# Attention behind two expert layers: when the transposes and the copy of a group's row maxima are issued

## The reference, cut to what matters

```python
x = L0_attn_x                                    # (1, 2048, 512) float32
x = x + 0.5 * _L0_ffn_ref(_layernorm(x), ...)    # 8 experts, top 2
x = x + _L0_attn_ref(_layernorm(x), wq, wk, wv, wo)
x = x + 0.5 * _L0_ffn_ref(_layernorm(x), ...)

# _L0_attn_ref: QH = 16 heads of HD = 32, KVH = 4 heads of keys and values
q = apply_rope(q, cos, sin); k = apply_rope(k, cos, sin)
attn = jnp.einsum('bhqd,bhkd->bhqk', q, k) / np.sqrt(HD)
mask = jnp.triu(jnp.ones((t, t), dtype=bool), k=1)
attn = jnp.where(mask[None, None], -jnp.inf, attn)
attn = jax.nn.softmax(attn, axis=-1)
out = jnp.einsum('bhqk,bhkd->bhqd', attn, v)
```

## Time and profile before

| | before |
|---|---|
| median of three runs | 1295.05 us |
| the three runs | 1291.39, 1296.23, 1295.05 us |
| the profiled execution's own time | 1291.39 us |
| its span | 1290.1 us |
| TensorE matmuls busy | 1198.4 us, 93% |
| TensorE weight loads busy | 778.3 us, 60% |
| VectorE busy | 891.7 us, 69% |
| ScalarE busy | 665.4 us, 52% |
| GpSimd busy | 599.7 us, 46% |
| mean granted TensorE clock | 0.987 of full |

### The profile page before, as it was taken

One profiled execution on the slowest core, in us unless ns is written; L12 is line 12 of the kernel. 1 busy time (PEld: TensorE's weight loads), 2 busy tenths in 40 slices (PEclk: granted clock), 3 DMA queues, 4 the chain that ended last, 5 costly groups with the idle time before them and its releaser, 6 DMA issues.

```text
span 1290.1 us, 22099 instructions
## 1 busy us (share of the span) xinstructions
PE 1198.4 (93%) x7406; PEld 778.3 (60%) x7413; DVE 891.7 (69%) x2100; ACT 665.4 (52%) x1321; POOL 599.7 (46%) x496
## 2 busy tenths in 40 slices
PE   4899999999998999999999999989999978999996
PEld 3578888758776555444545455545444446777774
DVE  7767777679996666476577677677763666666664
ACT  2545555436555554354456565456567853444442
POOL 4845444323210111001436457454764273888886
PEclk9899999999999999999999999999999999999998
DMA  9933333565630032023445844655843263666665
GB/s 331 364 97 107 106 108 108 169 178 107 101 57 5 32 68 35 1 69 67 98 99 147 173 108 99 197 120 146 162 98 67 69 236 85 102 106 101 101 103 78
DMA packets 68557, 148.52 MB, mean 115 GB/s; under 512 B 8832, under 2 KB 29312, under 8 KB 64448
## 3 DMA queue, kind: packets, MB, share of 16 engines
q0 software_dynamic: 35184, 93.34, 34.3%
q1 hardware_dynamic: 33264, 53.77, 12.2%
HBM read 81.28 MB, written 33.55 MB: 89 GB/s over the span
## 4 chain that ended last, share of the span: by engine, by line
PE 61%; DVE 15%; DMA 10%; issue 6%; POOL 4%; ACT 4%; SPq 0%; DVEq 0%; POOLq 0%; ACTq 0%
PE bank L839 10%; PE bank L1635 10%; PE bank L1647 9%; PE bank L997 8%; PE bank L862 6%; PE bank L1702 4%; PE bank L1665 4%; DMA XG<-xn,TK 4%; POOL out L789 3%; DMA out<-Y,DI 3%; DVE PM L1010 3%; DVE bank L1012 2%; PE bank L821 2%; PE bank L1398 2%; DMA CD<-P 1%
## 5 line engine op out<-in xcount | busy, mean ns | idle before, releaser
L1754 ACT ACTIVATE P<-bank 128x512 f32<-128x512 f32 (+3 forms) x640 | 303.6, 535 | 259.3 <-PE bank L1635 252.7
L1010 DVE TENSOR_REDUCE PM<-bank 128x1 f32<-128x512 f32 x384 | 252.8, 686 | 82.6 <-PE bank L997 81.9
L1635 PE MATMUL bank<-Qs,Ks 98*128 98x512 f32 (+3 forms) x640 | 241.0, 407 | 5.1 <-ACT P L1754 2.8
L997 PE MATMUL bank<-Ks,Qs 96*128 96x512 f32 (+3 forms) x640 | 234.4, 387 | 10.8 <-DVE PM L1012 5.3
L1635 PEld LDWEIGHTS bank<-Qs,Ks 98*128 98x128 f32 x640 | 116.8, 190 | 130.8 <-issue 59.5
L1813 POOL TENSOR_SCALAR_AFFINE_SELECT P<-P 128x512 f32<-128x512 f32 x64 | 42.7, 677 | 284.6 <-ACT P L1754 235.2
L1012 DVE CUSTOM_DVE_ANT_0 bank<-bank,KB 128x128 f32<-128x128 f32 (+3 forms) x256 | 124.7, 499 | 56.4 <-PE bank L997 55.8
L997 PEld LDWEIGHTS bank<-Ks,Qs 96*128 96x128 f32 x640 | 121.5, 191 | 57.5 <-DVE PM L1010 17.5
L1647 PE MATMUL bank<-P,V 128*32 128x512 f32 (+3 forms) x1280 | 150.9, 543 | 3.7 <-POOL P L1813 3.7
L1827 POOL TENSOR_TENSOR CH<-CH,P 128x512 f32<-128x512 f32 x108 | 139.2, 1435 | 14.1 <-ACT P L1754 13.3
L789 POOL DMA_INDIRECT out<-Y,DI x78 | 126.1, 1617 | 38.4 <-issue 29.4
(11 more groups left out here) (195 smaller groups left out, 1978.1 us busy)
## 6 DMA issues: line engine op xcount, KB each, us to landing
CD<-P POOLq DMA_DIRECT2D x17, 1024.0 KB, 7.3
xn<-XN SPq DMA_DIRECT2D x8, 1024.0 KB, 6.5
WR<-L_ffn_w POOLq DMA_DIRECT2D x16, 512.0 KB, 15.6
XO<-y POOLq DMA_DIRECT2D x8, 1024.0 KB, 9.6
WR<-L_ffn_w SPq DMA_DIRECT2D x16, 512.0 KB, 8.4
CD<-P SPq DMA_DIRECT2D x7, 1024.0 KB, 5.2
CD<-CH POOLq DMA_DIRECT2D x7, 1024.0 KB, 6.9
XA<-y POOLq DMA_DIRECT2D x24, 256.0 KB, 4.2
```

Of the source, the lines that this page charges most:

```text
L997: pe.matmul(bk(g, bank)[:, 0:n], g.Qs[b][0:96, G % 4 * 4 + h, c * P:c * P + P], g.Ks[0:96, G % 4, k * BQ:k * BQ + n], start=True, stop=Tru ...
L1010: dve.tensor_reduce(dst, bk(g, bank)[:, 0:n], AX.X, ALU.max).then_inc(s(f"free{bank}"), 1)
L1635: pe.matmul(bk(g, bank)[:, o:BQ], g.Ks[0:98, G % 4, k * P:k * P + P], g.Qs[G // 4][0:98, G % 4 * 4 + j, o:BQ], start=True, stop=True).then ...
L1754: act.activation(a.P4[buffer_of(n)][:, j, o:BQ], bk(g, score_bank(g, i))[:, o:BQ], ACT.Exp, scale=scale).then_inc(s("exp"), 1)
```

## The change

A group's transposes (`found`) are issued one place later: not behind the weigh at j = 3, but at j = 0 of the next tile, behind its first score and the tops that stand there. The copy (`foundcopy`) is issued one score further on, at j = 1. VectorE's `solvemax` stays where it was.

```diff
-    told, weight, given, extra, known, copying, free = 4, 0.0, 0.0, [], [], [], True
+    told, weight, given, extra, known, solved, turned, free = 4, 0.0, 0.0, [], [], [], [], True
@@
-            if copying:
-                plan.append(("foundcopy", copying.pop()))
+            if turned:
+                plan.append(("foundcopy", turned.pop()))
+            if solved:
+                turned.append(solved.pop())
+                plan.append(("found", turned[0]))
             if j == 1 and extra:
                 plan += extra.pop(0)
             if j == 3 and n:
                 if known and known[0][0] <= at and free and n - 1 not in LAST.values():
-                    copying.append(known.pop(0)[1])
-                    plan.append(("solvemax", copying[0]))
+                    solved.append(known.pop(0)[1])
+                    plan.append(("solvemax", solved[0]))
                 plan.append(("weigh", n - 1))
-                if copying:
-                    plan.append(("found", copying[0]))
```

## The result

The changed kernel's median is 1287.93 us (9 runs, 1285.94 to 1292.19) against 1295.05 us before, 7.1 us less. The ratio on record, which is estimated from all runs of both kernels and is not the ratio of the two medians (0.9945), is **0.9962, interval [0.9945, 0.9980]**, 4.9 us. So by the three readings the change makes the kernel faster by 0.1 to 0.4%, 1.5 to 4.9 us. The first shows the largest gain, and the third by itself can't be told from no change.

What follows compares the result with a forecast made beforehand. TensorE was taken to bound the attention stage, gaining only where it stands still. Cover 2.95, copy waits 0.7, group 6 -0.1 and group 8 0.8 sum to 4.35 us: 1295.05 - 4.35 = 1290.7 us, own range 1289 to 1293.

Steps and rivals of the forecast that it cites:

- the range that I gave 8 times in 10: Whole kernel: the median of the changed kernel lies between 1285.5 and 1296.5 us.
- the clock's rival: Behind group 8: less idling removes a fall of TensorE's clock, 1.7 us more gained, 1287 to 1289 us; chance 0.20.
- the sum of 4.35: Attention stage: all terms together, 2.95 + 0.7 - 0.1 + 0.8 us, taken off the time before.
- The cover of the wait: Groups 9 to 14: score and tops ahead of the transposes fill TensorE's wait for VectorE's maxima, 2.95 us.
- the two copy waits at groups 9 and 12: TensorE's wait for ScalarE's copy to free the transposes' bank goes there, 0.35 us each, 0.7 together.
- group 8's 0.8: Group 8: the 512-wide top ahead of the router's transpose goes out earlier and VectorE's chain moves up, 0.8 us.
- group 15's 0.18: Group 15: 0.18 us of covered wait, struck from the sum because TensorE soon waits 1.20 us for GpSimd.
- The wait itself: TensorE's transposes waiting for VectorE's last step of the maxima: from 5.8 to about 2.7 us, in five places.
- Groups 4 to 7 at nothing: No wait for the maxima to win there; copy waits at 5 and 7 stay, group 6 loses 0.1 us.
- Group 10's 0.35: Group 10: a score and the narrow top cover 0.35 of the 0.82 us wait for the maxima.
- Nothing gained: TensorE runs ahead but loses the gain waiting for banks VectorE has not freed; 1294 us, chance 0.20.
- The held-back copy: Twelve groups: copy behind two exponentials frees the bank 0.54 us later each, 6.5 us in all, 1297.2 us; chance 0.05.

Runs made afterwards that it cites:

- the three readings: The changed kernel against the kernel before, measured three times: ratios 0.9962, 0.9985 and 0.9988.
- the old place and the close copy: Kernel before with the transposes left behind the weigh and the copy right behind them, ahead of the next tile's first exponential: ratio 0.9967.
- the close copy: Changed kernel with the copy right behind the moved transposes, behind the tile's first exponential and not its second: ratio 0.9953 to the kernel before.

## Why the prediction was right, and where not

The median of 1287.93 us lies in the range that I gave 8 times in 10, but below my own range of the forecast, 1289 to 1293, and in the band of the clock's rival, 1287 to 1289. That rival is not what happened: the profiled executions of both kernels have 10.2 us at the low clock in the attention stage, and that stage is 4.3 us shorter, as the sum of 4.35 said. The other 3 us of the difference of the medians are not explained by the change, I call them luck, and so is how near the first ratio (4.9 us) comes to the sum, for the next two readings give 1.9 and 1.6 us. What bears the prediction out is the comparison place by place.

The time from solve to solve, from profiles in which the clock did not fall in that stretch ("fall" marks the one for which there was none such; the forecast is my term for the place):

| stretch | before, us | changed, us | difference | forecast |
|---|---|---|---|---|
| first score to group 4's solve | 31.41 | 31.50, 31.48 | +0.1 | 0 |
| 4 to 5 | 27.54 | 27.77 | +0.23 | 0 |
| 5 to 6 | 31.49 | 31.25 | -0.24 | 0 |
| 6 to 7 | 46.65 | 46.93 | +0.28 | +0.1 |
| 7 to 8 | 44.18 | 44.36 | +0.18 | 0 |
| 8 to 9 | 53.72 | 52.80 | -0.92 | -0.8 |
| 9 to 10 | 40.99 | 40.12 | -0.87 | -0.92 |
| 10 to 11 | 42.65, 42.68, 42.91 | 44.45, 44.51, 45.93 (fall) | +1.8 or more | -0.35 |
| 11 to 12 | 50.95 | 50.48 | -0.47 | -0.48 |
| 12 to 13 | 65.61 | 64.67 | -0.94 | -0.94 |
| 13 to 14 | 54.04 | 53.52 | -0.52 | -0.48 |
| 14 to 15 | 51.79 | 51.34 | -0.45 | -0.48 |
| 15 to the end | 28.93 | 28.94 | 0 | 0 |

Without the row of group 10 the differences sum to -3.6 us; the forecast's terms without that of group 10 sum to -4.0.

The mark itself moves a little at groups 4 to 8. VectorE's reduction writes into the bank that the transposes take, which is another one now. At group 5 the solve stands 1.15 us behind the start of the weigh beside it and stood 0.92 behind it before, at group 8 1.48 and 1.30. That the other bank comes free later is the likely cause and is not shown. From weigh to weigh instead of from solve to solve, the rows from 4 to 8 are +0.06, -0.08, +0.28 and +0.04, and that of group 8 is -0.74. From group 9 on the mark stands where it stood.

**The cover of the wait** held, place by place, within 0.05 us, but for group 10. So did the two copy waits at groups 9 and 12 (0.35 each, inside 0.92 and 0.94), and, within 0.1, group 8's 0.8. That group 15's 0.18 would be lost to GpSimd held too: the mask is waited for 1.23 us now, 1.20 before.

**The wait itself fell further than forecast**, to 1.6 us instead of 2.7. At group 12 it lost 0.78 us where the cover was put at 0.59. Half of the difference stands in the timeline: the score behind a weigh is followed only 0.34 us later (787.47 to 787.81), not 0.24. The first matmul behind one of another kind so takes 0.1 more until the next starts, and the change adds one such switch at each group: weigh, score, transposes, score instead of weigh, transposes, score. Where TensorE waits anyway the 0.1 is hidden in the wait. I took all added spacing for work done. The other half, some 0.1 us at groups 12 and 13, is open.

**Groups 4 to 7 at nothing was wrong by a little.** From weigh to weigh they cost 0.3 us together, where I had 0.1. With no wait to hide it, the added switch is paid, 0.1 at each. Against it stand the copy waits of groups 5 and 7, which I had expected to stay near 0.5: they were 0.56 and 0.26 us and are 0.29 and 0.21. Group 6's is 0.59 for 0.51. At group 4 there is also a new wait of 0.31 us, of the spread reciprocals for L1010:

```profile
453.41 1.08 PE L1683 MATMUL bank<-K,R 128*32 128x128 f32 x32 [0.31 <-DVE PM L1010]
```

These terms sum to nearly 0.5 and not to 0.3; the rest is open.

**Group 10's 0.35 was not seen in the end.** The step that failed there is the cover term of 0.35 us: I counted it in full, although a chain of transfers bounds the end of this stretch. GpSimd's additions by DMA for group 9 form a chain in which each waits for the landing of the one before. In the changed kernel, over this stretch:

```profile
685.21 0.86 POOL L1844 DMA_DIRECT2D CD<-P  x1 [0.84 <-ACT P L1755]
...
697.39 0.85 POOL L1844 DMA_DIRECT2D CD<-P  x1 [0.53 <-ACT P L1755]
...
710.53 0.86 POOL L1844 DMA_DIRECT2D CD<-CH  x1 [4.31 <-DMA CD<-P]
...
711.87 2.07 POOL L1814 TENSOR_SCALAR_AFFINE_SELECT P<-P 128x512 f32<-128x512 f32 x2
```

and in the kernel before:

```profile
689.73 0.86 POOL L1843 DMA_DIRECT2D CD<-P  x1 [0.82 <-ACT P L1754]
...
702.36 0.85 POOL L1843 DMA_DIRECT2D CD<-P  x1 [1.00 <-ACT P L1754]
...
714.67 0.86 POOL L1843 DMA_DIRECT2D CD<-CH  x1 [3.78 <-DMA CD<-P]
```

From the first to the last issue it is 25.3 us now and 24.9 before, though the middle issue, which waits for ScalarE and not for a transfer, comes 0.45 us sooner. The mask stands behind the last of them on GpSimd's queue, and TensorE behind the mask. So this stretch is bound by the landing of the middle transfer, and what TensorE wins ahead of it it waits out: 1.79, 1.82 and 1.82 us in the three profiles of the changed kernel, 1.83 with the change for groups 9 to 15 alone, against 1.26, 1.23 and 1.48 us before. I had checked this absorption for group 15 and not for group 10.

Why the middle transfer lands later though it is issued sooner shows in part. SyncE's load `XO<-L_attn_x`, also of 1 MB, stands behind the maxima's own two transfers on its queue and so behind the copy. It goes out at 697.50 now and 701.99 before, in both kernels 4.00 us behind group 10's solve, and the two transfers are under way together. The last number is the us from issue to landing, first of the changed kernel, then of the kernel before:

```profile
CD<-P POOLq DMA_DIRECT2D x1, 1024.0 KB, 12.6
XO<-L_attn_x SPq DMA_DIRECT2D x1, 1024.0 KB, 8.7
...
XO<-L_attn_x SPq DMA_DIRECT2D x1, 1024.0 KB, 6.5
CD<-P POOLq DMA_DIRECT2D x1, 1024.0 KB, 11.8
```

With the old place and the close copy the load goes out 3.29 us behind the solve; the addition is issued at 4.13, later than in the changed kernel (3.89), and yet lands 15.0 us behind the solve for 16.5, TensorE has no wait for the mask there, and the stretch takes 41.52. So in this stretch the copy's place seems to count more than the transposes', by way of this load. That is argued from these rows; no run moved the load alone.

**The clock was a rival that looked in the wrong place.** I looked for a fall that goes, behind group 8. What the profiles show is one that comes, behind group 10's longer stand:

```profile
712.00:713.00 1.00, 0.00 (x0) 0.00 (x0) 0.43 (x1) 0.19 (x1) 1.00 (x3) 1.00 1.10 213
713.00:714.00 1.00, 0.49 (x4) 0.23 (x8) 0.00 (x0) 0.00 (x0) 0.94 (x2) 0.71 1.05 213
...
716.00:717.00 1.00, 1.00 (x7) 0.78 (x4) 0.00 (x0) 0.26 (x2) 0.00 (x0) 0.58 1.06 115
```

TensorE stood still in the us from 712 and has the lower level from 713.4 to 716.8. A fall stands at this place in all five profiles in which group 10's transposes had moved and the copy stood one score behind (3.4, 3.4, 6.8 and 6.8 us long, and 10.2 with the solve moved too), and in none of seven with the transposes in their old place there. With the close copy the order there is the same up to the copy, the stand is 1.11 us, there is no fall, and the stretch takes 42.00; one score further the stand is 1.59, again without a fall. That is an association over these profiles; no run put the stand and the clock apart.

With the fall the stretch is 1.8 us longer than before (44.48 against 42.68), and 3.2 when the fall is twice as long, so the second half of it costs 1.4. How the 1.8 divide between the fall and the longer stand no profile shows.

These 1.8 to 3.2 us are lost against the 3.6 won, but they can't be the whole reason that the second and third readings are near 0.9987. The three profiles of the changed kernel all have this fall, and with it and all others their attention stage takes 570.1, 569.5 and 571.1 us against 574.4, 574.8 and 573.8 before, still 4 us less on the mean. Outside the attention stage, where nothing was changed, the three profiles of the kernel before take 714.4 to 715.9 us and the three of the changed one 716.6, 719.3 and 717.1, 2.3 more on the mean. So in the profiled executions about half of the gain is given back where the change does nothing. Three profiles of each can't tell whether that is chance, and the cause stays open.

**The rivals.** "Nothing gained" is out: the tops' waits for VectorE's maxima did not grow (0.7 us for L1010 before and now), the one new wait of the kind being the 0.31 us at group 4. The held-back copy is out for the change, whose chain from the transposes' start to the copy's end stays at 1.93 us (1.6 at group 4), as it was before (my 1.97 reached to the start of the top that waited), but it is real as a mechanism: held some 0.5 to 0.6 us longer, it costs 0.28% by itself. The Trainium skill, "Perfetto Trace Analysis", "Identifying the Most-Contended Engine", judges TensorE not by matmul busy time but by weight-load busy time and by the share of its peak arithmetic that is used. By the first of these, 52%, read as the prediction reads it, nothing should have been gained; the stretches without a fall, 3.6 us shorter together, disagree.

**What to run.** The transposes moved and the copy right behind them, 0.9953, or both one score further, 0.9940, beat the kernel before. In one series with the changed kernel (0.9985) only the first was measured. Against the changed one, its stretches behind groups 5, 6 and 10 are 30.76, 46.21 and 42.00 us instead of 31.25, 46.93 and 44.5.

## What to carry to other kernels

When a producer and a consumer in two in-order queues meet, put work that needs neither between them on the consumer's queue, and leave the producer where it is; moving both cost 14 us more here. Then look at what the handed-over buffer is still held for: placing its release one instruction nearer was worth about as much as the move, and one instruction farther cost about as much again. A gain ahead of a transfer can be given back where the transfer lands, so check each stretch for what bounds its end, not only the last one. And a gain of a few us in a stretch can be lost in the noise of the rest: compare the stretches as well as the total.

## What was unexpected of the hardware

Behind the first matmul of another kind the next one starts 0.10 us later than in a run of like ones (0.34 to 0.24 us between starts, score behind weigh, then a top). A low-clock piece of 3.4 us costs nothing where TensorE would have waited (behind group 13's solve, 53.99 us for 54.04) and 1.5 us where it would not (behind group 8's, 55.23 for 53.73); two profiles of the same kernel differ in the place of one or two such pieces, which is about the size of this change. A transfer of 1 MB (the middle one behind group 10) takes 12.6 us from issue to landing when it is issued 0.1 us ahead of another one of 1 MB, and 11.8 to 12.0 when 0.4 us behind it, so issuing it sooner brought nothing.
